# Graph and expert kernel: the down projection's weights kept expert by expert, and small tensors laid out anew

## The reference

```
h = x @ hasher_w.T ; sim = h @ keys.T          # 256 experts
vals, idx = top_k(sim, 4) ; w = softmax(vals)
for k in range(4):
    proj = silu(x . values_down[idx[k]])       # [1024, 32] each
    out += (proj . values_up[idx[k]]) * w[k]   # [32, 1024] each
x = x + (x_norm + out * scale)
```

## Time and profile before

| | |
|---|---|
| time, median of 3 runs | 777.37 us (776.72 to 777.39) |
| the profiled execution | 777.37 us, of which the span from first to last instruction is 775.6 us |
| TensorE clock granted, mean of the span | 0.971 of full speed |
| PE busy / DVE / ACT / POOL | 725.1 / 519.4 / 352.9 / 190.9 us |
| read from memory | 112.74 MB |
| expert loop, one group | 22.67 us, 14 of them alike |

### The profile page before, as it was taken

The page is one execution under the profiler, slowest core; times in us unless marked ns, Lnnn a source line. Parts: engine busy times, 40 slices in busy tenths (PEclk is TensorE's granted clock), DMA queues, the critical chain, the costliest instruction groups (busy, mean ns, idle before and its releaser), DMA issues.

```text
span 775.6 us, 9683 instructions
## 1 busy us (share of the span) xinstructions
PE 725.1 (93%) x3305; PEld 572.6 (74%) x3305; DVE 519.4 (67%) x833; ACT 352.9 (45%) x391; POOL 190.9 (25%) x333
## 2 busy tenths in 40 slices
PE   3999999997979998779999999999999999999998
PEld 3777776775655666547877888888888888888886
DVE  6897686688999999926588654445545444554543
ACT  3755889636535442112454534334443433444340
POOL 7203577798898604000000000000000000000000
PEclk9999999999989998868999999999999999999999
DMA  8775233350020013202843635665454566544421
GB/s 316 281 306 199 109 108 110 109 216 1 1 109 1 2 54 120 109 1 108 288 146 109 217 137 187 216 216 176 152 190 154 193 216 216 166 162 180 165 86 55
DMA packets 50059, 114.22 MB, mean 147 GB/s; under 512 B 2245, under 2 KB 35397, under 8 KB 44906
## 3 DMA queue, kind: packets, MB, share of 16 engines
q1 hardware_dynamic: 49418, 112.95, 40.9%
q0 software_dynamic: 160, 0.66, 0.2%
q10 hardware_dynamic: 448, 0.20, 0.1%
HBM read 112.74 MB, written 1.05 MB: 147 GB/s over the span
## 4 chain that ended last, share of the span: by engine, by line
PE 65%; POOL 15%; DVE 8%; issue 7%; ACT 4%; DVEq 1%; ACTq 0%; POOLq 0%
PE ps L1205 19%; PE ps L1207 18%; PE ps L1206 18%; POOL peak L496 5%; POOL pen L501 4%; POOL oh_src L498 4%; PE ps L1175 3%; DVE wlo L741 2%; DVE oh_dst L1034 2%; PE ps L1488 1%; PE ps L1521 1%; ACT chunk_col L597 1%; PE ps L1196 1%; ACT chunk_gap L592 1%; ACT whi L540 1%
## 5 line engine op out<-in xcount | busy, mean ns | idle before, releaser
L741 DVE TENSOR_TENSOR wlo<-raw,whi 128x2048 fp32r<-128x2048 f32 x104 | 236.0, 2292 | 72.9 <-ACT whi L540 71.5
L540 ACT ACTIVATE whi<-raw 128x2048 fp32r<-128x2048 f32 x104 | 196.1, 1911 | 99.8 <-PE ps L1207 94.8
L1205 PE MATMUL ps<-whi,nT_hi 128*128 128x512 f32 x424 | 170.7, 403 | 3.8 <-DVE wlo L741 2.4
L1206 PE MATMUL ps<-whi,nT_lo 128*128 128x512 f32 x424 | 167.0, 394 | 0.0
L1207 PE MATMUL ps<-wlo,nT_hi 128*128 128x512 f32 x424 | 166.9, 394 | 0.0
L931 DVE SCALAR_TENSOR_TENSOR ps<-ps,xt 128x1024 f32<-128x1024 f32 x80 | 97.7, 1221 | 4.8 <-PE ps L1229 4.5
L1205 PEld LDWEIGHTS ps<-whi,nT_hi 128*128 128x128 f32 x424 | 80.7, 190 | 22.5 <-DVE wlo L741 2.9
L1205 PE MATMUL ps<-whi,gT_hi 128*128 128x512 f32 x240 | 93.6, 390 | 0.0
L1207 PEld LDWEIGHTS ps<-wlo,nT_hi 128*128 128x128 f32 x424 | 80.7, 190 | 17.3
L1207 PE MATMUL ps<-wlo,gT_hi 128*128 128x512 f32 x240 | 93.4, 389 | 0.0
L1206 PE MATMUL ps<-whi,gT_lo 128*128 128x512 f32 x240 | 93.4, 389 | 0.0
(11 more groups left out here) (236 smaller groups left out, 869.3 us busy)
## 6 DMA issues: line engine op xcount, KB each, us to landing
raw<-n_L_ffn_values_down_dram SPq DMA_DIRECT2D x16, 2048.0 KB, 8.3
raw<-in_L_ffn_values_up_dram SPq DMA_DIRECT2D x16, 2048.0 KB, 7.5
raw<-in_L_gnn_W_hh_dram SPq DMA_DIRECT2D x8, 1024.0 KB, 9.1
raw<-in_L_gnn_W_oo_dram SPq DMA_DIRECT2D x8, 1024.0 KB, 5.8
raw<-in_L_gnn_W_ho_dram SPq DMA_DIRECT2D x8, 1024.0 KB, 4.8
raw<-in_L_gnn_W_hn_dram SPq DMA_DIRECT2D x8, 1024.0 KB, 5.2
raw<-in_L_gnn_W_on_dram SPq DMA_DIRECT2D x8, 1024.0 KB, 4.8
xt<-in_x_dram SPq DMA_DIRECT2D x4, 512.0 KB, 5.6
```

The costliest lines, as they stand in the source:

```text
L540: nc.scalar.activation(half(whi, s, j, down), half(raw, s, j, down), ACT.Copy)\
L741: nc.vector.tensor_tensor(half(wlo, s, j, down), half(raw, s, j, down), half(whi, s, j, down).bitcast(F32), ALU.subtract)\
L1205: nc.tensor.matmul(o, a_hi, b_hi, start=start, stop=False)
L1206: nc.tensor.matmul(o, a_lo, b_hi, start=False, stop=False)
```

## The change

Two edits. The halves of a down unit keep the layout of `raw` in `whi` and `wlo`: for each expert n a run of 128 elements (4 chunks of 32 columns) is read and written, and PE's moving operand becomes `[:, c, :, :]`, 16 runs of 32 elements that lie 256 elements apart. And `small` is replaced by eight tensors of their own, `scale_b` and `ba_b` further down the list, while `gT_hi` and `gT_lo` are declared after `gw` instead of before `top`. In the other helpers nothing changes; `half` without `down=True` gives what it gave.

```diff
--- before.py
+++ after.py
@@ -107,15 +107,17 @@
         nT_lo = sb("nT_lo", [P, C, PADN], F32R)
         iota = sb("iota", [P, N])
         iota16 = sb("iota16", [P, N], F16)
-        small = sb("small", [P, 48])
-        node, block_pos, rel_neg, spare, row_no, scale_b, ba_b = (
-            small[:, a:b] for a, b in ((0, 2), (2, 6), (6, 7), (7, 8), (8, 9), (9, 10), (10, 11)))
-        sel_ones = small[0:5, 11:12]
+        node = sb("node", [P, 2])
+        block_pos = sb("block_pos", [P, 4])
+        rel_neg = sb("rel_neg", [P, 1])
+        spare = sb("spare", [P, 1])
+        row_no = sb("row_no", [P, 1])
         ident = sb("ident", [P, P])
         ident16 = sb("ident16", [P, P], F16)
         ones16 = sb("ones16", [P, P], F16)
         below16 = sb("below16", [P, P], F16)
         sel = sb("sel", [5, 5, P], F32R)
+        sel_ones = sb("sel_ones", [5, 1])
         with ExitStack() as beside:
             win_rows = sb("win_rows", [P, 4, ROW], I32, beside)
         bias_hi = sb("bias_hi", [5, D], F32R)
@@ -131,6 +133,8 @@
         slot_idx = sb("slot_idx", [P, 2, WN])
         slot_idx16 = sb("slot_idx16", [P, 2, WN], F16)
         bucket_first = sb("bucket_first", [P, NBK])
+        scale_b = sb("scale_b", [P, 1])
+        ba_b = sb("ba_b", [P, 1])
         stats = sb("stats", [P, NT, 2, 6])
         mv = sb("mv", [P, NT, 2])
         ln = sb("ln", [P, 5, NT])
@@ -203,8 +207,6 @@
             zT_lo = sb("zT_lo", [P, C, PADZ], F32R, late)
 
         hT_sb = sb("hT_sb", [2 * PD, N])
-        gT_hi = sb("gT_hi", [P, BLOCKS, N], F32R)
-        gT_lo = sb("gT_lo", [P, BLOCKS, N], F32R)
         top = sb("top", [P, NT, 8])
         topi = sb("topi", [P, NT, 8], U32)
         topf = sb("topf", [P, NT, 8])
@@ -213,6 +215,8 @@
         route = sb("route", [P, NT, XP])
         act_g = sb("act_g", [P, NT, GX * PD])
         gw = sb("gw", [P, NT, GX * PD])
+        gT_hi = sb("gT_hi", [P, BLOCKS, N], F32R)
+        gT_lo = sb("gT_lo", [P, BLOCKS, N], F32R)
 
         ps = ctx.enter_context(nc.psum_tensor("ps", [P, 8 * HALF], F32))
 
@@ -350,12 +354,9 @@
 
         def half(t, s, j, down=False):
 
-            flat = t[:, s, j * UNIT // 2:(j + 1) * UNIT // 2]
-            if not down:
-                return flat
-            if t is raw:
-                return t[:, s, :].rearrange("p (n c w) -> p c n w", n=GX, c=C)[:, 4 * j:4 * j + 4, :, :]
-            return flat.rearrange("p (c n w) -> p c n w", c=4, n=GX)
+            if down:
+                return t[:, s, :].rearrange("p (n k) -> p n k", n=GX)[:, :, j * 4 * PD:(j + 1) * 4 * PD]
+            return t[:, s, j * UNIT // 2:(j + 1) * UNIT // 2]
 
         def tokens(t3, c, t):
 
@@ -1530,14 +1531,14 @@
             new_nodes(zT_hi, zT_lo, messages, 18, False)
             new_nodes(zT_hi, zT_lo, messages, 19, False, stop=True)
 
-            down_hi, down_lo = ([w[:, s, :].rearrange("p (c n w) -> p c (n w)", c=C, n=GX) for s in range(2)]
+            down_hi, down_lo = ([w[:, s, :].rearrange("p (n c w) -> p c n w", n=GX, c=C) for s in range(2)]
                                 for w in (whi, wlo))
             t_cols = [slice((2 + 2 * t) * NH, (4 + 2 * t) * NH) for t in range(NT)]
 
             def down_part(s, c, t):
 
                 return three(bank(4 + t), nT_hi[:, c, t_cols[t]], nT_lo[:, c, t_cols[t]],
-                             down_hi[s][:, c, :], down_lo[s][:, c, :], start=c == 0, stop=c == C - 1)
+                             down_hi[s][:, c, :, :], down_lo[s][:, c, :, :], start=c == 0, stop=c == C - 1)
 
             def down(g, within=None):
 
@@ -1579,12 +1580,12 @@
                 if c % 4 == 0:
                     pe.wait_ge(lo_ready[0], 2 * SLOT_W + c // 4 + 1)
                 for w in (down_hi, down_lo):
-                    nc.tensor.matmul(bank(4), nT_hi[:, c, t_cols[0]], w[0][:, c, :], start=c == 0 and w is down_hi,
+                    nc.tensor.matmul(bank(4), nT_hi[:, c, t_cols[0]], w[0][:, c, :, :], start=c == 0 and w is down_hi,
                                      stop=False)
             turn(1, 1)
             pe.wait_ge(turned_lo, NT + 1)
             for c in range(C):
-                nc.tensor.matmul(bank(4), nT_lo[:, c, t_cols[0]], down_hi[0][:, c, :], start=False, stop=c == C - 1)
+                nc.tensor.matmul(bank(4), nT_lo[:, c, t_cols[0]], down_hi[0][:, c, :, :], start=False, stop=c == C - 1)
 
             for part, (aT, there) in enumerate(((nT_hi, turned_hi), (nT_lo, turned_lo))):
                 pe.wait_ge(there, 2 * NT)
```

## The result

The changed kernel takes 791.57 us (median of 6 runs) beside 776.94 us for the kernel before; the ratio is 1.0184, 95% interval 1.0170 to 1.0199, so 14.3 us slower by the ratio. (One of the six, at 906.7 us and a mean clock of 0.745, is left out of the ratio.) The forecast was 777.4 us with a range up to 787.0: it missed. The profiled execution took 790.35 us, span 788.6.

A forecast was written before the change was run, and what follows sets the result against it. PE's own matmul rate was taken to bound the expert-group loop. Runs, splits and addresses were each put at 0 on a profiled run of 777.37 us, giving 777.4 us, with an eight-in-ten range of 775.4 to 787.0 us.

The forecast's parts named there:

- PE's pace alone bounds the loop: Expert-group loop: only PE's own rate counts, 96 matmuls at 226.7 ns plus 8 transposes making a pass of 22.67 us.
- (b): Splits at lines 540 and 741 in 128-element runs: 0 taken, at worst 34 ns a half, 0.14 us before the loop.
- (a): 768 down matmuls read their moving operand in 16 runs: 0 taken, between 8.2 us won and 13.4 us lost.
- (c): New addresses of the small tensors and gT: 0 taken, at most 0.85 us; chance of more 0.02 faster, 0.01 slower.
- Sum: Whole kernel: (a), (b) and (c) at 0 on a profiled run of 777.37 us, forecast 777.4 us, chance 0.64.
- Jumps cost PE time: Moving read of the 768 down matmuls, nowhere else: slower, 782.0 to 790.8 us, middle near 786; chance 0.22.
- The range: Whole kernel, eight in ten: 775.4 to 787.0 us, holding the forecast and jump prices up to 0.83 ns.
- The signs to watch: Profile after: down starts, pass against 22.67 us, split durations, and changes before 388 us or in up matmuls, meaning addresses.

The follow-up runs named there:

- the first experiment: The kernel before with the new layout of the down units alone, every tensor at its old address: 785.48 us, ratio 1.0112.

## Why the prediction was wrong

- *PE's pace alone bounds the loop*: right, and the reason why nanoseconds showed. Every ns of a start is 0.77 us for the down product and 0.72 for the up product.
- *(b) The splits cost nothing*: right. 2284 to 2294 and 1902 to 1922 ns after; and the kernel in which PE alone reads in runs has the whole loss of the layout.
- *(a) "The down matmuls read their moving operand in runs ... I take 0"*: the first step that failed. It was +11.0 ns x 768 = 8.4 us. The neighbour that was chosen, line 1478's fp16 stream, shares the run length but neither the element size nor the weight load: it loads 64 columns of fp16, a quarter of the bytes, and its load takes 106 to 110 ns against 188 (min/median/max below, from the trace before). Which of these makes it cheap was not tried. The price was sought in the jumps; the runs put it in the addresses of the runs modulo 256, since the same 15 jumps cost 0 at one step and 11 ns at another.

```profile
L1478 PEld LDWEIGHTS ps<-head_dst,head_src x8: 106/108/110, 319.5 to 320.8; 128*64 128x64 f16 x8
```

- *(c) "No row shows an address to matter ... I take 0"*: the second, and the worse, since it had 0.03 of the chance. It looked at the weight load's own time, 188 ns under 226.7, and called that cover. The load's time did not change, 188 ns after as well; the matmul that streams beside it took longer. Measured: 7.5 ns x 720 for `gT`, 7 ns x 144 for `zT`, about 5 ns x 144 for the features and `gT_last`, 7.1 us by these; 784.13 us was measured for the addresses alone, 7.3 us above its 776.82.
- *Sum*: 8.4 + 7.1 = 15.5 us by the starts, 14.3 by the ratio. The 13 passes of the profiled executions lost 11.3 us where the starts give 13 x 0.89 = 11.5; the parts before 443 us are mostly hidden.
- *The rival "Jumps cost PE time"* came near the time with its top of 790.8 us by accident. For the layout alone it had place and size right: its middle was near 786 us, and the first experiment took 785.48. Its "nowhere else" is refuted by the up product's 234.2 ns, and its cause by the 15 jumps that cost nothing when they keep step.
- *The range* up to 787.0 us was put together from rivals taken one at a time. Either half of the change alone (785.48 and 784.13 us) lies inside it; both together do not.
- *The signs to watch* were good: "A change before 388 us or in the up matmuls would have to come from addresses" is what the timeline showed first.

Of the two rules of the Trainium skill that were weighed, "SBUF Cachelines" ("Advanced Engine Details and Errata") gave 0 for the runs, and "PSUM Cachelines", read over to the moving side, gave a loss for every jump; the runs measured 8.4 us with one step and 0 with another, so neither holds here. A third bears on what was found: "SBUF — State Buffer", section "Who interferes with whom", gives PE two independent read ports, one for the moving operand and one for weight loads, and says that PE waits on nobody. The measurement decides against reading that as free of charge: 226.7 to 234.2 ns for matmuls of one form, as the starts of their two reads were moved against each other.

What stays open is the mechanism. The runs show that equal starts modulo 256 are fast, that unequal ones are slower in most products, and that an unchanged load time goes with a slower stream; that both reads meet in the same memory was only argued. Why 16 and 64 bytes are cheap is not known, nor what makes one pass fast and the next slow at a distance of 4 or 240. Within a product the distance is the same to a matmul's own weights and to those of its neighbours, so the runs do not tell which of the two loads counts. Unequal distances for `hi` and `lo`, other weight widths, and 2-byte types were not tried.

## What to carry to other kernels

Where back-to-back fp32r matmuls set the pace, keep the start of the stationary and of the moving operand equal modulo 256 bytes, in each matmul (another distance that looks cheap in one run may be at the slower pace in the next pass); declaring a small tensor ahead of a large one is enough to lose it, and padding got it back for `gT` here. A moving operand in runs was free where its address kept step with one piece modulo 256 (tried: runs of 256 bytes at steps of 1024, and runs of 128 bytes at steps of 384); runs of 128 bytes at steps of 512 or 1024 cost 11 ns a matmul. And a change that "only" moves declarations is to be priced like any other: list the starts before and after.

## What was not expected of the hardware

Averaged over a product, matmuls of 512 fp32r columns never came faster than one in 226.6 ns at full clock, where the columns alone are 213.3 ns at 2.4 GHz. The excess depends on addresses: 13.3 ns at best, 20.9 at a distance of 160 bytes, 24.7 with runs out of step, while the listed weight load stays at 188 ns on the mean (187 to 190 by group, in all the runs). At two distances the same instructions ran at either of two paces, pass by pass. The loss also shows in listed durations (389, 396, 401 ns), so a table of groups by line and tensor finds it where the stamps of single starts are too coarse.
